# First FFN's weights loaded and split inside the first FFN stage, with x loaded in pieces

## The reference

```python
x = x + 0.5 * ffn0(norm(x)); x = x + rwkv(norm(x)); x = x + 0.5 * ffn0(norm(x))
x = x + 0.5 * ffn1(norm(x)); x = x + mamba(norm(x)); x = x + 0.5 * ffn1(norm(x))
```

## Time and profile before

| | before |
|---|---|
| runs shown, us | 782.3, 785.05, 785.35 (median 785.05) |
| the profiled execution, us | 779.87 |
| its span, first to last instruction, us | 778.2 |
| mean granted TensorE clock | 0.951 |
| PE busy | 686.9 us (88%) |
| DVE busy | 568.3 us (73%) |
| ACT busy | 414.7 us (53%) |
| POOL busy | 323.1 us (42%) |

### The profile page before, as it was taken

One profiled execution on the slowest core, in us unless ns is written; L12 is line 12 of the kernel. 1 busy time (PEld: TensorE's weight loads), 2 busy tenths in 40 slices (PEclk: granted clock), 3 DMA queues, 4 the chain that ended last, 5 costly groups with the idle time before them and its releaser, 6 DMA issues. The chain is left out here.

```text
span 778.2 us, 12435 instructions
## 1 busy us (share of the span) xinstructions
PE 686.9 (88%) x4044; PEld 511.1 (66%) x4044; DVE 568.3 (73%) x1289; ACT 414.7 (53%) x747; POOL 323.1 (42%) x404
## 2 busy tenths in 40 slices
PE   0889995668789999999999697999999994999997
PEld 0667774234356777777778586677777773677785
DVE  3688866889978788888988636456565575689775
ACT  2456585857415555556655336455555551555553
POOL 1357784020316566555666416122212201357354
PEclk9999998879999999999999769899999996999999
DMA  5245530000003322212223000000000000223132
GB/s 155 82 151 150 181 110 0 1 0 0 1 0 111 109 94 86 91 60 81 83 81 84 1 1 1 1 3 1 0 0 0 0 2 0 85 80 103 61 96 68
DMA packets 32757, 43.10 MB, mean 55 GB/s; under 512 B 5184, under 2 KB 15424, under 8 KB 32704
## 3 DMA queue, kind: packets, MB, share of 16 engines
q1 hardware_dynamic: 32704, 42.46, 17.7%
HBM read 41.13 MB, written 1.31 MB: 55 GB/s over the span
## 5 line engine op out<-in xcount | busy, mean ns | idle before, releaser
L558 POOL TENSOR_TENSOR p_prod<-p_p,p_gate_row 128x512 f32<-128x512 f32 x128 | 200.1, 1572 | 126.3 <-DVE p_p L417 68.4
L320 ACT ACTIVATE p_sil<-p_ps_a 128x512 f32<-128x512 f32 x176 | 105.1, 597 | 132.7 <-PE p_ps_a L100 126.9
L422 DVE TENSOR_TENSOR p_hlo<-p_prod,p_hhi 128x512 fp32r<-128x512 f32 x176 | 150.5, 856 | 3.0 <-ACT p_hhi L329 2.7
L417 DVE TENSOR_TENSOR p_p<-p_sil,p_ps_b 128x512 f32<-128x512 f32 x128 | 87.3, 682 | 58.6 <-ACT p_sil L320 47.2
L329 ACT CAST p_hhi<-p_prod 128x512 fp32r<-128x512 f32 x176 | 108.0, 614 | 24.1 <-POOL p_prod L558 24.1
L98 PE MATMUL p_ps_acc<-p_hhi,w_downhi 128*128 128x512 f32 x176 | 71.9, 409 | 3.0 <-DVE p_hlo L422 2.9
L98 PE MATMUL p_ps_a<-xt_hi,w_uphi 128*128 128x512 f32 x176 | 74.5, 423 | 0.0
L98 PE MATMUL p_ps_b<-xt_hi,w_uphi 128*128 128x512 f32 x176 | 71.3, 405 | 0.4 <-DVE p_prod L417 0.4
L100 PE MATMUL p_ps_a<-xt_hi,w_uplo 128*128 128x512 f32 x176 | 70.3, 399 | 0.0
L99 PE MATMUL p_ps_a<-xt_lo,w_uphi 128*128 128x512 f32 x176 | 70.2, 399 | 0.0
L100 PE MATMUL p_ps_b<-xt_hi,w_uplo 128*128 128x512 f32 x176 | 70.2, 399 | 0.0
(11 more groups left out here) (300 smaller groups left out, 1436.5 us busy)
## 6 DMA issues: line engine op xcount, KB each, us to landing
p_gate_row<-gate_rows SPq DMA_DIRECT2D x128, 256.0 KB, 3.3
w_rawbuf<-in_L_ffn_fc_w_dram SPq DMA_DIRECT2D x3, 512.0 KB, 5.6
w_rawbuf<-in_L_ffn_w_dram SPq DMA_DIRECT2D x3, 512.0 KB, 6.5
out_dram<-x SPq DMA_DIRECT2D x4, 256.0 KB, 3.6
w_rawbuf<-in_L_ffn_shared_w_dram SPq DMA_DIRECT2D x3, 256.0 KB, 6.3
mb_xraw<-in_L_attn_W_B_dram SPq DMA_DIRECT2D x1, 512.0 KB, 4.4
mb_xraw<-in_L_attn_W_C_dram SPq DMA_DIRECT2D x1, 512.0 KB, 5.0
gate_rows<-p_gates_t SPq DMA_DIRECT2D x16, 16.0 KB, 1.4
```

Of the source, the lines that this page charges most:

```text
L320: nc.scalar.activation(sil[:, u % 2], ps_a[:, u % 2], ACT.Silu).then_inc(c["sil"].sem, 1)
L417: nc.vector.tensor_tensor(dst, sil[:, u % 2], ps_b[:, u % 2], ALU.mult).then_inc(c["p1"].sem, 1)
L422: nc.vector.tensor_tensor(hlo[:, u % R], prod[:, u % R], hhi[:, u % R].bitcast(F32), ALU.subtract).then_inc(c["hlo"].sem, 1)
L558: G.tensor_tensor(prod[:, u % R], p1[:, u % 2], gate_row[:, e % ROWS], ALU.mult).then_inc(c["prod"].sem, 1)
```

## The change

The setup block is gone. The first FFN stage gets an `opening`: ffn0's raw weights and `x` are loaded, and the weights split, inside its own block.

- SP loads the first quarter of `x`, then three groups of weights (shared gate and up, router, first experts' up), the second quarter of `x`, the other three groups (shared down, other experts' up, experts' down), and the other half of `x`. The bias goes with a later load.
- The raw weights of ffn0 land in the raw buffers of ffn1's weights. SP therefore waits, ahead of the load of ffn1's first groups, until all six groups of ffn0 are split (`raw_lo` at 6).
- ACT and DVE do the six splits at written-out places of the prologue. On DVE `measure(1)` and `measure(2)` come later than before, on POOL `scale(2)`.
- PE waits for the splits that each product needs.
- `filled` now counts the four constant instructions on POOL; PE and DVE wait for it once.

```diff
@@ ffn_stream, tensor engine
+                if n == 0 and u in (2, 6):
+                    split_up_to(3 if u == 2 else 5)
...
+                if n == 0 and u in (0, 2):
+                    split_up_to(4 if u == 0 else 6)
...
+            if opening:
+                pe.wait_ge(c["filled"].sem, c["filled"].at(4))
             if not begun:
                 turn_x(0)
+            split_up_to(2)
             route(0)
@@ scalar engine
+            for k in range(3):
+                own(k)
             if not begun:
                 high_x(0)
+            own(3)
             take_logits(0)
             gate(0, 0)
             tanh(0)
             gate(0, 1)
+            own(4)
             gate(0, 2)
+            own(5)
             take_gates(0)
@@ vector engine
             if not begun:
+                landed(0)
                 measure(0)
+                own(0)
+                own(1)
                 normal(0)
-                measure(1)
+                own(2)
+                if not opening:
+                    measure(1)
                 low_x(0)
+                if opening:
+                    landed(1)
+                    measure(1)
+            own(3)
             normal(1)
...
             for u in range(3):
                 gated(0, u)
+            if opening:
+                landed(2)
+                measure(2)
             low(0, 0)
             low_x(1)
+            own(4)
             gated(0, 3)
             low(0, 1)
+            own(5)
@@ gpsimd
             if not begun:
                 scale(0)
                 scale(1)
-            scale(2)
+            if not opening:
+                scale(2)
             weights(0)
+            if opening:
+                scale(2)
@@ sync
                     if between and e == ROWS:
+                        if opening:
+                            sp.wait_ge(c["raw_lo"].sem, c["raw_lo"].at(OWN))
                         between(sp)
...
+            if opening:
+                own, source = opening
+                def take(k, some):
+                    sp.dma_start(x[:, some], source[:, some]).then_inc(c[f"x{k}"].sem, 16)
+                take(0, slice(0, BT))
+                own.load(sp, slice(0, 3))
+                take(1, slice(BT, 2 * BT))
+                own.load(sp, slice(3, None))
+                take(2, slice(2 * BT, TILES))
@@ program
+        raw = w1_set.raws
+        places = [raw[0][:, 0:S], raw[2], raw[3], raw[1][:, 0:S], raw[4], raw[5]]
+        w0_set = RawWeights(None, counts, "w0", [w0_jobs[k] for k in (0, 2, 3, 1, 4, 5)], one_semaphore=False, raws=places)
-        setup()
```

More of the change, by code:

```diff
@@ L108, in __init__, with ffn_stream @@
         self.units, self.shared = weights.units, weights.shared
-def ffn_stream(nc, tag, counts, spare, sb, ps, x, xt, consts, kinds, gate_dram, norm, loads=(), splits=(), out_dram=None, entry=None, begun=False, heads=False):
+def ffn_stream(nc, tag, counts, spare, sb, ps, x, xt, consts, kinds, gate_dram, norm, loads=(), splits=(), out_dram=None, entry=None, begun=False, heads=False, opening=None):
     splits = split_jobs(splits)
+    OWN = len(opening[0].jobs) if opening else 0
     LEAD, BEHIND = 4, 2
@@ L128, in ffn_stream @@
     HEADED = BLOCKS + 2 if heads else BLOCKS
+    POOL_SPLITS, DVE_SPLITS = [{at: tuple(OWN + k for k in some) for at, some in t.items()} for t in (POOL_SPLITS, DVE_SPLITS)]
     SPLITS = {**POOL_SPLITS, **DVE_SPLITS}
@@ L386, in next_rows, with own @@
                     last.then_inc(c["r_tok"].sem, 1)
+            def own(k):
+                if opening:
+                    split_hi(nc, act, c, splits[k])
+            for k in range(3):
+                own(k)
             if not begun:
                 high_x(0)
+            own(3)
             take_logits(0)
@@ L603, in body @@
                         scale_norms(nc, pool, c, consts, entry, NEXT_SCALES[n, p])
+            if opening:
+                G.memset(consts["ident"][:], 0.0).then_inc(c["filled"].sem, 1)
+                G.memset(consts["minus_half"][:], -0.5).then_inc(c["filled"].sem, 1)
+                G.iota(rank[:], [[0, BT], [1, EXPERTS]], base=0, channel_multiplier=0,
+                       allow_small_or_imprecise_dtypes=True).then_inc(c["filled"].sem, 1)
+                pool.wait_ge(c["filled"].sem, c["filled"].at(3))
+                G.affine_select(out=consts["ident"][:], in_=consts["ident"][:], compare_op=ALU.not_equal, fill=1.0, base=0,
+                                pattern=[[-1, P]], channel_multiplier=1).then_inc(c["filled"].sem, 1)
             if not begun:
@@ L665, in ffn_stream @@
         c["io"].base += 16 * NBLK
+    if opening:
+        c["filled"].base += 4
     c["raw_hi"].base += len(splits)
@@ L2048, in program @@
         names = ("a b sil p1 hhi hlo prod row0 row1 row2 row3 store stored down route xn xt xhi xlo lg lgs lgt gth gates gt gts acc_s ot out "
-                 "stats moments veps rstd score gap key top hot share g12 filled io raw0 raw1 raw2 raw3 raw4 raw5 raw_hi raw_lo rw_raw w1_raw mb_raw").split()
+                 "stats moments veps rstd score gap key top hot share g12 filled io raw0 raw1 raw2 raw3 raw4 raw5 raw_hi raw_lo x0 x1 x2 rw_raw w1_raw mb_raw").split()
         counts = {n: Count(sem("s_" + n)) for n in names}
@@ L2133, in program @@
             vectors.append((rw["tmrow"][:, q], a["L0_attn_" + n].rearrange("q r p -> q (r p)").broadcast_to([P, P])))
+        vectors.append((bias[:], a["L1_ffn_expert_bias"].rearrange("(a e) -> a e", a=1).broadcast_to([P, EXPERTS])))
         rw_set = RawWeights(None, counts, "rw", [
@@ L2183, in mamba_stage @@
+        S = w0.shared
+        raw = w1_set.raws
+        places = [raw[0][:, 0:S], raw[2], raw[3], raw[1][:, 0:S], raw[4], raw[5]]
+        w0_set = RawWeights(None, counts, "w0", [w0_jobs[k] for k in (0, 2, 3, 1, 4, 5)], one_semaphore=False, raws=places)
+        w1_set.arrived = [(count, total + used) for (count, total), (_, used) in zip(w1_set.arrived, w0_set.arrived)]
         def mamba_stage():
@@ L2219, in program @@
                            loads=(lambda sp: w1_set.load(sp, slice(0, 4)), load_rest, mb.load) if k == 0 else (),
-                           splits=(w1_set,) if k == 0 else (mb,) if later == "mamba" else (), heads=later == "mamba", entry=entry if k == 0 else None, begun=k > 0 and STAGES[k - 1] == "rwkv",
+                           opening=(w0_set, x_dram) if k == 0 else None,
+                           splits=(w0_set, w1_set) if k == 0 else (mb,) if later == "mamba" else (), heads=later == "mamba", entry=entry if k == 0 else None, begun=k > 0 and STAGES[k - 1] == "rwkv",
                            out_dram=out_dram if k + len(stages) == len(STAGES) else None)
```

56 lines of the change are left out of this document (16 added, 40 removed).

## The result

The changed kernel took 775.45 us (median of 4 runs, 773.18 to 777.06) beside 785.2 us (4 runs, 782.3 to 785.67) for the kernel before: ratio 0.988, 95% interval 0.985 to 0.992. Repeated later beside 11 other runs of the kernel before, it took 775.65 us (6 runs) against 782.46: 0.992, interval 0.988 to 0.995. One execution of the kernel before in a later series took 3651.62 us and is left out of the medians and ratios here. The gain is between 7 and 10 us, and the forecast of 776.1 lies 0.65 from the first median.

What follows compares the result with a forecast made beforehand. The start was taken as a chain of latencies and the rest of the stage as PE's. The terms -11.4 + 2.5, others 0, gave -8.9 us: 785.05 to 776.1, range 772.5 to 781.5.

Steps and rivals of the forecast that it cites:

- Step 1: Kernel start: with a quarter of x loaded first, the first router matmul comes at 11.1 instead of 22.53, -11.4 us.
- Step 2: DVE's measure(1) after the first split of x: hidden, as the key waited for PE until 26.46 anyway; 0 us.
- Step 3: ACT's two weight casts ahead of the first block's gates delay their copy, store and gate rows by 1.4 us.
- Step 4: SP's wait for the last split and ffn1's loads delay gate row 4 and the second block's gates, +2.5 us in all.
- Step 5: TensorE's clock does not fall behind PE's 3.1 us idle before the second block's gates: 0, bounds 0 and +1.5 us.
- No later slack takes it in, nor is a gain lost in one: First stage: a delay up to 46 us delays everything, so the 8.9 us lead should stand at the stage's end.
- the bias moves to a queue with time: Among the other edits: the bias's load, moved to a later queue, costs nothing; 0 us.
- full exclusion, and the clock falls: Rival at the fifth row: sixth split waits a whole POOL product, PE idles 3.8 us, clock falls; -6.7, 778.3; chance 0.27.
- Row 4 is cheap: Rival at the fifth gate row: it lands by 44.7 or sooner, only step 3 counts; -10.0, 775.0 us; chance 0.15.
- the two rivals of the front: x's quarter lands when whole x did, -6.3, 778.7, chance 0.08; late load stops ACT before the gates, 789.0, chance 0.03.

Runs made afterwards that it cites:

- r_before: The kernel before with no edit, run and profiled again; 782.88 us (12 runs), ratio 1.001.
- e_early: e_both with the fifth split moved ahead of the second normalization and the sixth's cast behind the first silu; 770.09 us, ratio 0.984 to the kernel before.
- e_rows_first: Changed kernel with ffn1's first five loads and SP's wait for the last split behind all eight gate rows of the first block; 772.6 us, 0.987 to the kernel before.
- e_own_raws: Changed kernel with ffn0's raw weights in places of their own, so ffn1's first loads need no wait, order kept; 773.01 us, 0.989 to the kernel before.
- e_both: Changed kernel with the edits of e_rows_first and e_trickle together; 768.83 us, ratio 0.982 to the kernel before.
- r_after: The changed kernel with no edit, run and profiled again; 775.65 us (6 runs), ratio 0.992 to the kernel before.
- e_trickle: Changed kernel with the 14 small vectors and the bias issued behind the second block's gate rows instead of in SP's list; 772.27 us, 0.986 to the kernel before.
- e_before_trickle: The kernel before with only the edit of e_trickle, small loads spread over the second block's gate rows; 781.07 us (12 runs), ratio 0.998.
- e_best: e_both with ACT's casts of the fifth and sixth group moved behind the copy of the gates; 768.58 us, ratio 0.983 to the kernel before.
- e_x_whole: Changed kernel with x loaded whole ahead of all weights instead of a quarter first; 779.42 us (12 runs), ratio 0.995 to the kernel before.

## Why the prediction was right, step by step

The time was right, in part by luck, and so was most of the first 30 us; two statements on what comes after were wrong.

**Step 1, the start of the chain: right.** Statistics at 3.85 (forecast 4.5), normalization at 7.19 (7.4), router at 10.96 (11.1): 11.57 us gained of a forecast 11.4. x landed 0.65 earlier than taken, and `norm_rstd`, 0.5 longer behind DVE's subtraction, gave most of that back.

**Step 2, measure(1): right.** The key came at 15.52, 10.94 before the 26.46 of the earlier trace rows, the start's gain but for 0.6. That 0.6 is not `measure(1)`: from the router's first matmul to the key r_before takes 4.56 us as after does, and the profile of before took 3.93 because PE's matmuls followed each other faster from 2.9 us on.

**Step 3, two casts ahead of the gates: right in time, its size less.** The copy of the gates at 19.84, forecast 19.8. PE's matmul ahead of it stands at 18.55, so the copy follows it by 1.29 us where it followed by 0.31 before (29.50, 29.81): the casts cost 1.0 and not 1.4. The 0.6 of step 2 made up for it, which is luck.

**Step 4, the fifth row: the mechanism was right, its size too small.** Its first half erred on the cautious side. The sixth split was forecast stretched by 0.6 and took its plain 1.22 us, because DVE got in first (24.46) and POOL's row landed in the middle of it (24.86). ACT's cast of the product starts at 26.87, 1.19 behind the subtraction's end at 25.68, where it starts 1.33 after POOL in e_early. So it was POOL that waited. The same distance, 1.18 to 1.20, stands behind the subtraction in e_rows_first, e_own_raws and e_both, whenever POOL's product had started. The Trainium skill, page "SBUF — State Buffer", section "SBUF: two separate sides", says that whichever of a VectorE operation with two SBUF inputs and a GpSimd operation starts first keeps the ports for its whole length; these rows agree with it, and the rival built on it only had the order of the two wrong. The subtractions of the earlier trace rows had been misread in the prediction. In the trace of before POOL's second product stands at 36.10 to 37.39 and the third starts at 37.36 and takes 1.74 us instead of 1.29. DVE's subtraction of 36.88 arrived in the middle of the second, ended at 37.94, 0.55 behind its end, and the third ended 1.16 behind that. A wait for the rest of a product lengthens DVE's row by that rest only, so 1.06 and 1.18 do not speak for a partial stretch. One pair of rows does not fit the words "whole length": in e_rows_first `norm_rstd` runs from 5.29 to 6.33, and a subtraction of DVE starts in it at 5.56 and takes its plain 0.69. ffn1's loads went out at 25.70, a microsecond before the forecast 26.7. The second half took more than it back: from that first issue the five loads and the row took 35.23 - 25.70 = 9.5 us, where the step's term has 45.8 - 38.1 = 7.7 (1.4 until traffic, 5.0 of bytes, 1.3 to land). The row's delay on the shifted clock is 35.23 + 11.57 - 43.31 = 3.5 us instead of 2.5, inside the bounds of 1.4 and 4.7. The lead at the second block's gates was 7.84, not 8.9. e_rows_first and e_own_raws confirm the place: counted from the copy of the first block's gates, the second block's come 2.1 to 2.3 earlier without the loads in front of the row, and 0.8 to 1.1 without the wait alone. Against r_before the term is right as it stands: its fifth row is used at 44.88, that of r_after at 35.28, 2.3 later on the shifted clock (11.86).

**Step 5, the clock: wrong.** "I take no fall, just below the row that fell" was a guess between an idle of 1.99, behind which the clock stayed, and one of 3.19, behind which it fell. The idle became 3.47, past both, and the clock fell; but the forecast 3.1 would not have saved it either, since it fell behind 2.77 and 2.68 too. The cost is 1.4 us by the marks (24.82 - 23.43) and 1.7 by the mean clock, about the step's upper bound of 1.5; in r_after, with 0.52 over 6 us, it is more (25.66 us from the second block's gates to the third's).

**"No later slack takes it in, nor is a gain lost in one" and "the bias moves to a queue with time": wrong.** The distance did not stand at the end of the stage: it was 4.4 instead of 8.9. One microsecond of the miss is step 4's (8.9 to 7.84), 1.4 the clock's (to 6.45), and 2.0 (to 4.4) arise behind the third block's gates, at the list of 20 issues that SP has between the rows of the second block and the gates of the third. In r_before and r_after that last part is 0.9. e_trickle beside e_before_trickle shows that the list costs more in the changed kernel. By the rows above it is the list's own length and the longer wait behind it, not an early start that ran into it: the bias was given no cost in the prediction ("a queue with time"), and the queue it moved to had none. What was argued from PE's waits missed this, because SP's list already reached PE before the change, in a wait of 0.60 and no more.

**Why the total was right all the same.** By the marks of the two profiles the lead at the stage's end was 4.4 us, by those of r_before and r_after 7.7, by the medians the gain is 6.8 to 9.75. The executions of the kernel before differ at the same place: r_before lost the clock at its own fifth row and ended the stage 3.5 us behind the profile that the sum was made on. The sum of 8.9 was too large against that profile and was then set against a median that is itself 5.2 above it. So two errors of some microseconds each met. Two of three profiles of the kernel before show the fall there; how often it comes in all its executions was not measured. The rival "full exclusion, and the clock falls" (778.3) comes nearest to what the trace shows in mechanism: a fall, the row 3.5 late instead of its 3.2, though POOL was blocked and not DVE. "Row 4 is cheap" fell, and so did the two rivals of the front.

## What to carry to other kernels

When a load is moved to "later", look at the queue it moves to, and at what stands behind it there. A list of small DMA issues on SP at some 0.48 us each cost 1.1 to 1.6 us before and 2.5 to 3.2 after, with one load more in it, and it is mended by dealing the issues out behind transfers that are waited for anyway. A wait of PE costs twice where it is long enough to lower the clock (2.68 us and more in these traces), so a row that is needed soon goes ahead of weights that are not. And before a sum made on one profile is set against a median, look whether that profile is typical at the very place of the change.

## What had not been expected of the hardware

- The granted clock behind PE's wait for the second block's gates was 1.00 after idles of 1.42 and 1.43 us (e_rows_first, e_both, e_early, e_best) and 1.99 (before). It fell, to 0.72 or less on the mean of 5 to 6 us, after 2.68 (e_own_raws), 2.77 (r_before), 2.98 (e_before_trickle), 3.38 (e_trickle), 3.47 (after), 3.67 (e_x_whole, 0.50) and 3.73 (r_after, 0.52). What the waits ended is the same product of POOL in all.
- The runs of one kernel follow its mean granted clock: the 12 of r_before go from 779.57 us at 0.953 to 786.9 at 0.938. That a part of the spread is the number of such falls fits this, but is not shown: only profiled executions show where the clock fell.
- PE's first matmuls of 512 columns follow each other every 0.43 us and later every 0.23, and the switch comes 2.9 us behind the router's first matmul in the profile of before, 3.3 in e_rows_first, 4.9 in after and 5.0 in r_before. It moves the first block's gates by half a microsecond and more.
- A product of POOL that meets a subtraction of DVE in progress ends nearly a whole product (1.2 us) after it, and `norm_rstd` on POOL, four numbers per partition, took 1.54 us instead of 1.04 behind one. The other way round, a subtraction that started inside `norm_rstd` was not held up (e_rows_first, 0.69 us).
- The store of 16 KB of the first block's gates and the wait for it took 1.51, 1.88 and 2.42 us in three kernels, from one issue to the next, and 1.51 and 1.89 in two executions of the changed kernel; what makes the difference is open. For the third block it is 2.66 and 2.67 us in two profiles of before, and 3.32 to 3.35 in the five profiles in which the bias is issued right ahead of the store.
